# GpSimd zeroes the query buffer's lower rows, and the first layer norm is made in two halves

## The chip, the cores and the metric

One Trainium2 chip, one core of it. The time is the device time of one execution in microseconds (us). The kernel is launched once and does everything on that core.

## What is computed

The input x has 8 sequences of 512 tokens of 128 numbers (float32). Four sublayers follow one another, each as x = x + f(layernorm(x)): a linear attention with 16 heads, a mixture of 8 experts, a causal softmax attention whose heads share one key and value, and a filter in frequency space. Only the first is touched by the steps below:

```python
def _layernorm(x, axis=-1, eps=1e-05):
    m = jnp.mean(x, axis=axis, keepdims=True)
    v = jnp.var(x, axis=axis, keepdims=True)
    return (x - m) / jnp.sqrt(v + eps)
...
    x = x + _L0_attn_ref(_layernorm(x, axis=-1), L0_attn_w, L0_attn_w_out)
    x = x + _L0_ffn_ref(_layernorm(x, axis=-1), L0_ffn_router_w, L0_ffn_w1, L0_ffn_b1, L0_ffn_w2, L0_ffn_b2)
    x = x + _L1_attn_ref(_layernorm(x, axis=-1), L1_attn_w_attn, L1_attn_w_proj)
    x = x + _L1_ffn_ref(_layernorm(x, axis=-1), L1_ffn_w_freq_real, L1_ffn_w_freq_imag, L1_ffn_bias)
```

## The kernel before, in words

Each engine has its own list of instructions, written by hand in one order, and semaphores tie the lists together. B is 8 sequences, P 128 partitions, NT 4 tiles of 128 tokens for each sequence, D 128.

**Start.** SyncE issues the loads of x (four sequences, then the constants, then the other four; lines 184 to 190) and then of the expert weights. ScalarE issues ten loads of small weights (L214). GpSimd's first work is `start_signals` (L176 to L182): it raises 110 semaphores one by one, in two lots, with s_started raised to 1 (LIN) after the first lot and to 2 (ALL) after the second. VectorE zeroes the lower 64 partitions of two buffers, `kTm` (L2134) and `qT` (L2135). These are used only by the third sublayer, hundreds of microseconds later. The instruction for `qT` writes 12288 words of four bytes in each of 64 partitions.

**The first layer norm.** VectorE then makes mean and variance of all 8 sequences, two sequences at a time (`dve_sequences`: eight BATCH_NORM_STATS2 at L292, a wait, eight BATCH_NORM_AGGREGATE at L297; four times). It adds epsilon for all of them in one small instruction that writes the tile `sd` (L306). ScalarE, which has loaded the table of the square root while it waited (an `act_preset` at L269 is a one-element activation that makes the table load happen), takes the root (L316) and then loads the table of the exponential. VectorE goes on with `prep_dve`: it copies the transposed weights out of PSUM (L247 to L253), waits for TensorE's next products (L233 to L236) and copies these (L256, L258). Only then it takes the reciprocal (L310) and the product of it with minus the mean, the tile `shift1` (L2144). ScalarE's `xln` (L464, normalised x, four tiles) waits for that.

**The linear attention.** TensorE transposes `xln` of sequence 0 (L601), ScalarE copies the result (L470), TensorE multiplies by the weights (L611), ScalarE makes `kx` and `qv` out of it (L481, L482), VectorE the largest query of each head, `qmax` (L367), GpSimd adds to the keys (L533), and TensorE sums the keys (L621, L622). Then there is one turn for each sequence (`dve_lin_turn`, `act_lin_turn`, `pe_lin_turn`, `pool_lin_turn`), turn b doing the sums of sequence b and the start of sequence b+1. `act_lin_turn` of turn b ends with the `xln` of sequence b+2. GpSimd's list from `lin_pool` on begins with L533 of sequence 0.

Of the kernel before, what the change touches and what calls it, by code (L numbers as in the profile page):

```python
# [17 lines left out]
ALU = mybir.AluOpType  # L18
# [3 lines left out]
P = 128  # L22
# [26 lines left out]
def build(nc, x_in, w_qkv, w_out, router_w, w1, b1, w2, b2, w_attn, w_proj, wf_re, wf_im, f_bias,  # L49
# [15 lines left out]
    with ExitStack() as ctx:  # L65
# [177 lines left out]
        def prep_dve(dve):  # L243
            dve.wait_ge(s_c.sem, s_c.total(16))
            nc.vector.tensor_copy(ident_bf[:, :], ident).then_inc(s_idb.sem, 1)
            dve.wait_ge(s_prep_t.sem, s_prep_t.total(1))
# [25 lines left out]
        ln_ve, ln_sd, ln_rstd = signal("ln_var_eps"), signal("ln_std"), signal("ln_rstd")  # L272

        class LayerNorm:


            def __init__(self, tag, nth):
                self.nth = nth
# [20 lines left out]

            def dve_rstd(self, dve):  # L300
                self.dve_var_eps(dve, B)
                self.dve_inverse(dve)

            def dve_var_eps(self, dve, turns):
                dve.wait_ge(self.mv.sem, self.mv.total(turns))
                nc.vector.tensor_scalar(sd[:, :, :], mv[:, :, :, 1], EPS, None, ALU.add).then_inc(self.ve.sem, 1)  # L306

            def dve_inverse(self, dve):
                dve.wait_ge(self.sd.sem, self.sd.total(self.nth))
                nc.vector.reciprocal(rstd[:, :, :], sd[:, :, :]).then_inc(self.rstd.sem, 1)  # L310
                dve.wait_ge(self.rstd.sem, self.rstd.total(self.nth))

            def act_std(self, act):
                act_preset(act, ACT.Sqrt)
                act.wait_ge(self.ve.sem, self.ve.total(self.nth))
                nc.scalar.activation(sd[:, :, :], sd[:, :, :], ACT.Sqrt).then_inc(self.sd.sem, 1)  # L316

        ln1, ln2, ln3, ln4 = (LayerNorm(f"ln{n}", n) for n in range(1, 5))

# [192 lines left out]
        def lin_act(act):  # L512
# [337 lines left out]
        def route_act(act):  # L850
            act_preset(act, ACT.Exp)
            act.wait_ge(s_shift.sem, s_shift.total(2))
            act_route_xln(act, 0, 0)
# [475 lines left out]

        def dve_inverse(dve, lo, hi, nth):  # L1330
            dve.wait_ge(ln_sd.sem, ln_sd.total(nth))
            nc.vector.reciprocal(rstd[:, lo:hi, :], sd[:, lo:hi, :]).then_inc(ln_rstd.sem, 1)
            dve.wait_ge(ln_rstd.sem, ln_rstd.total(nth))

        def act_std(act, lo, hi, nth, preset=True):
            if preset:
                act_preset(act, ACT.Sqrt)
            act.wait_ge(ln_ve.sem, ln_ve.total(nth))
            nc.scalar.activation(sd[:, lo:hi, :], sd[:, lo:hi, :], ACT.Sqrt).then_inc(ln_sd.sem, 1)

        def dve_filter_xln(dve, j):
# [80 lines left out]
        def dve_end_xln(dve, half):  # L1422
            part, to = x_sb[:, SEQ[B - 1], end_tiles(half), :], fx[:, (B - 1) % 2, end_tiles(half), :]
            token = lambda a: a.unsqueeze(2).broadcast_to([P, END_TILES, D])
            dve.wait_ge(ln_sd.sem, ln_sd.total(7 + half))
            nc.vector.reciprocal(rstd[:, B - 1, end_tiles(half)], sd[:, B - 1, end_tiles(half)]).then_inc(ln_rstd.sem, 1)
            nc.vector.tensor_tensor(to, part, token(mv[:, B - 1, end_tiles(half), 0]), ALU.subtract).then_inc(f_c.sem, 1)
            dve.wait_ge(ln_rstd.sem, ln_rstd.total(7 + half))
            dve.wait_ge(f_c.sem, f_c.at(B - 2, half + 1))
# [13 lines left out]
        def act_end_std(act, half):  # L1443
            act.wait_ge(ln_ve.sem, ln_ve.total(7 + half))
            nc.scalar.activation(sd[:, B - 1, end_tiles(half)], sd[:, B - 1, end_tiles(half)], ACT.Sqrt).then_inc(ln_sd.sem, 1)
# [51 lines left out]
        def act_end_xln(act):  # L1497
            act.wait_ge(s_shift.sem, s_shift.total(5))
            act.wait_ge(f_xTp.sem, f_xTp.at(B - 4, 1))
# [106 lines left out]
        def dve_turn(dve, b, tail=True, middle=True, front=True):  # L1606
            for s in range(STEPS):
                for place in PLACES:
# [14 lines left out]
                    if b == B - 1 and (s, place) == (0, "A"):  # L1623
                        dve_inverse(dve, 0, IN_LAST_TURN, 5)
                    if b == B - 1 and place == "A" and s in XLN_AT:
# [10 lines left out]
        def mqa_dve(dve):  # L1636
# [4 lines left out]
            dve_moe_add(dve, last_scatter(SEQ[1]), SEQ[1])  # L1641
            dve_inverse(dve, 0, 1, 3)
            dve_ln3_shift(dve, 0, 1)
# [10 lines left out]
            dve_max(dve, 0, range(2), bank_at_start)  # L1654
            dve_inverse(dve, 1, B, 4)
            dve_ln3_shift(dve, 1, B)
# [8 lines left out]
            dve_var_eps(dve, ln4, B - 2, B - 1)  # L1665
            dve_inverse(dve, B - 2, B - 1, 6)
            dve_end_shift(dve)
# [107 lines left out]
        def act_turn(act, b, tail=True, middle=True, front=True):  # L1775
            for s in range(STEPS):
# [10 lines left out]
                if (b, s) == (STD_TURN, STD_STEP):  # L1787
                    act_std(act, 0, IN_LAST_TURN, 5)
                    act_preset(act, ACT.Exp)
# [17 lines left out]

        def mqa_act(act):
            act_std(act, 0, 1, 3)
            act.wait_ge(s_shift.sem, s_shift.total(3))  # L1810
            act_xln(act, 0)
# [6 lines left out]
            act_first_kT(act, 0)  # L1818
            act_std(act, 1, B, 4, preset=False)
            act_preset(act, ACT.Exp)  # L1820
            act.wait_ge(s_shift.sem, s_shift.total(4))
            act_xln(act, 1)
# [286 lines left out]
        @block.scalar  # L2109
        def _(act):  # L2110
            prep_act(act)
            act.wait_ge(s_started, LIN)
            act.wait_ge(s_c.sem, s_c.total(16))
            ln1.act_std(act)
            act_preset(act, ACT.Exp)
            lin_act(act)
            act.wait_ge(s_started, ALL)
            ln2.act_std(act)
            route_act(act)
            moe_act(act)  # L2120
            mqa_act(act)
# [91 lines left out]
```

## Time and profile before

| | before |
|---|---|
| median of 3 runs | 795.57 us (793.87 to 795.86) |
| span of the profiled execution | 801.9 us |
| TensorE busy in it | 644.6 us (80%) |
| VectorE busy | 548.5 us (68%) |
| ScalarE busy | 353.9 us (44%) |
| GpSimd busy | 361.2 us (45%) |

The only time of the profiled execution itself that is at hand is its span, from its first to its last instruction, and that is 6.3 us more than the median of the three runs. In the chain of work that ended last, the shares of the span are TensorE 45%, VectorE 20%, GpSimd 13%, waiting for nothing that the profile shows 12%. The first sublayer fills about the first 205 us. In the names of the engines, PE is TensorE's matmul, PEld its weight load, DVE VectorE, ACT ScalarE, POOL GpSimd and SP SyncE; a "q" behind a name is its queue. An arrow in brackets names what ended the idle time of the engine just before the row.

### The profile page before, as it was taken

The page shows a single profiled execution, that of the slowest core. Times are in us where ns is not written, and L with a number is a line of the kernel's source. Part 1 is how long each engine was busy: PE and PEld are TensorE (multiplying, and loading weights), DVE is VectorE, ACT ScalarE, POOL GpSimd, SP SyncE. Part 2 cuts the span into 40 slices and gives each one's busy share as a digit, 9 for nine tenths or more (in the row PEclk, how much of TensorE's full clock was granted, in tenths as well). Part 3 has the DMA queues.
Part 4 walks back from the last instruction along what each step waited for, and adds up shares of the span by engine and source line. Part 5 has one row for each costly group of instructions (what it writes and reads, how often), then busy time and mean ns, then how long its engine had stood idle before and what let it go on. Part 6 is the DMA issues. An engine that isn't in the chain of part 4 may idle for free.

```text
span 801.9 us, 14622 instructions
## 1 busy us (share of the span) xinstructions
PE 644.6 (80%) x4312; PEld 398.9 (50%) x4345; DVE 548.5 (68%) x1808; ACT 353.9 (44%) x764; POOL 361.2 (45%) x513
## 2 busy tenths in 40 slices
PE   1489898997206699999795569899999999999795
PEld 1246666664103478877584223454545454544453
DVE  8378888888691133243336797889898989898454
ACT  0323232320711222233231205776777777767883
POOL 0176555552007587788862102434434344333342
PEclk9999999999657799999997667999999999999998
DMA  9300000000231222223324440203131221300011
GB/s 297 106 1 1 0 1 0 0 1 1 78 106 49 32 43 41 41 42 43 44 25 102 52 59 4 60 16 50 26 41 31 34 41 25 50 15 2 17 54 40
DMA packets 42937, 33.51 MB, mean 42 GB/s; under 512 B 4144, under 2 KB 39520, under 8 KB 42864
## 3 DMA queue, kind: packets, MB, share of 16 engines
q1 hardware_dynamic: 32528, 24.62, 14.3%
q0 software_dynamic: 8992, 7.38, 6.4%
q8 instruction: 35, 0.57, 0.3%
q10 hardware_dynamic: 1344, 0.62, 0.3%
q14 instruction: 38, 0.31, 0.2%
HBM read 13.87 MB, written 8.91 MB: 28 GB/s over the span
## 4 chain that ended last, share of the span: by engine, by line
PE 45%; DVE 20%; POOL 13%; issue 12%; ACT 3%; DMA 2%; SPq 1%; DVEq 0%; ACTq 0%; POOLq 0%
PE bank L1982 8%; DVE masked L1574 7%; POOL x_dram L950 7%; POOL x_row L943 6%; PE wide L1969 5%; PE wide L639 4%; PE bank L1914 3%; PE bank L611 3%; PE wide L640 3%; PE bank L1121 2%; DVE st L292 2%; DVE mx L1574 2%; DVE prod L389 2%; PE wide L621 1%; PE bank L1994 1%
## 5 line engine op out<-in xcount | busy, mean ns | idle before, releaser
L1761 ACT ACTIVATE pexp<-wide 128x512 f32<-128x512 f32 (+2 forms) x384 | 181.3, 535 | 73.4 <-PE wide L1969 70.2
L1685 POOL TENSOR_SCALAR_AFFINE_SELECT pexp<-pexp 128x256 f32<-128x256 f32 x256 | 106.1, 418 | 185.7 <-ACT pexp L1761 183.7
L1574 DVE CUSTOM_DVE_ANT_0 masked<-bank,mask_qk 128x384 f32<-128x384 f32 (+3 forms) x356 | 154.0, 481 | 18.6 <-PE bank L1914 17.7
L1969 PE MATMUL wide<-qT,kTe 128*128 128x256 bf16 (+3 forms) x501 | 119.7, 301 | 6.6 <-ACT pexp L1761 2.5
L1092 ACT ACTIVATE hT<-wide,b1T 128x512 f32<-128x512 f32 x64 | 43.8, 687 | 147.1 <-PE wide L1112 112.8
L1914 PE MATMUL bank<-kTm,qT 128*128 128x384 bf16 (+3 forms) x348 | 87.1, 318 | 18.9 <-DVE mx L1574 9.4
L950 POOL DMA_INDIRECT x_dram<-yg,row_u x48 | 76.2, 1588 | 31.5 <-DVE yg L999 18.6
L1574 DVE CUSTOM_DVE_ANT_0 masked<-wide,mask_qk 128x256 f32<-128x256 f32 (+3 forms) x156 | 74.2, 498 | 17.8 <-PE wide L1914 17.8
L943 POOL DMA_INDIRECT x_row<-xln_dram,row_u x64 | 62.4, 975 | 52.8 <-DVE slot_tok L819 33.6
L1982 PE MATMUL bank<-pexp,vx 128*32 128x512 f32 (+3 forms) x1024 | 83.9, 439 | 0.5 <-POOL pexp L1685 0.5
L1121 PE MATMUL bank<-w_sb,hT 128*128 128x128 f32 x512 | 71.6, 283 | 5.0 <-issue 5.0
L1121 PEld LDWEIGHTS bank<-w_sb,hT 128*128 128x128 f32 x512 | 66.2, 197 | 17.2 <-issue 16.1
L565 POOL TENSOR_TENSOR kv<-kx,qv 128x1024 f32<-128x1024 f32 x32 | 62.4, 1951 | 24.2 <-PE wide L640 24.2
L1112 PE MATMUL wide<-xgT,w_sb 128*128 128x512 f32 x128 | 69.2, 628 | 2.8 <-DVE xgT L982 1.6
L1969 PEld LDWEIGHTS wide<-qT,kTe 128*128 128x128 bf16 x512 | 48.5, 99 | 41.5 <-ACT pexp L1761 21.6
L1914 PEld LDWEIGHTS bank<-kTm,qT 128*128 128x128 bf16 x356 | 30.8, 102 | 66.5 <-DVE mx L1574 48.4
L389 DVE TENSOR_TENSOR prod<-wide,qs 128x1024 f32<-128x1024 f32 x32 | 38.9, 1217 | 11.6 <-PE wide L640 9.0
L1982 PEld LDWEIGHTS bank<-pexp,vx 128*32 128x32 f32 x1024 | 25.9, 109 | 40.2 <-issue 28.4
L639 PE MATMUL wide<-kv,cst 128*128 128x512 f32 x64 | 35.7, 640 | 10.4 <-DVE prod L389 10.3
L1574 DVE DVE_READ_ACCUMULATOR2_ANT mx<- 128x1 f32 x512 | 42.6, 83 | 0.0
L996 DVE TENSOR_TENSOR yg<-bank,b2rep 128x512 f32<-128x512 f32 x16 | 11.1, 691 | 44.8 <-PE bank L1121 40.9
L398 DVE TENSOR_REDUCE y_in<-prod 128x128 f32<-128x1024 f32 x32 | 38.9, 1216 | 3.9 <-PE bank L664 3.4
(273 smaller groups left out, 1056.0 us busy)
## 6 DMA issues: line engine op xcount, KB each, us to landing
qT<-qp SPq DMA_DIRECT2D x144, 64.0 KB
x_sb<-in_L_attn_x SPq DMA_DIRECT2D x8, 256.0 KB, 6.7
w_sb<-in_L_ffn_w SPq DMA_DIRECT2D x1, 2048.0 KB, 13.3
xln_dram<-rx SPq DMA_DIRECT2D x8, 256.0 KB, 2.3
out_x<-x_sb SPq DMA_DIRECT2D x7, 256.0 KB, 2.3
x_dram<-x_sb SPq DMA_DIRECT2D x6, 256.0 KB, 3.6
x_sb<-x_dram SPq DMA_DIRECT2D x6, 256.0 KB, 2.8
x_row<-xln_dram,row_u POOLq DMA_INDIRECT x64
```

The source lines that it names most:

```text
L565: nc.gpsimd.tensor_tensor(kv[:, k % 2, :].rearrange("p (h m l) -> p h m l", l=L, m=L), kx[:, par, k, :].rearrange("p (h l) -> p h l", l=L) ...
L639: nc.tensor.matmul(wide[:, 0:512], tri, kv[:, k % 2, 0:512], start=True, stop=True)
L943: nc.gpsimd.indirect_dma_start(out=x_row[:, e % 2, b, :], out_offset=None, in_=xln_dram, in_offset=bass.IndirectOffsetOnAxis(ap=row_u[:, b ...
L950: nc.gpsimd.indirect_dma_start(out=x_dram, out_offset=bass.IndirectOffsetOnAxis(ap=row_u[:, b * E + e:b * E + e + 1], axis=0), in_=yg[:, e ...
L1112: nc.tensor.matmul(psH[n % 3], w1_sb[:, e, c * P:(c + 1) * P], xgT[:, half, :], start=True, stop=True).then_inc(m_hp, 1)
L1121: ins = nc.tensor.matmul(psYe[half][:, j * D:(j + 1) * D], hT[:, half, c, j * P:(j + 1) * P], w2_sb[:, e, c, :], start=c == 0, stop=c == H ...
L1574: ins = nc.vector.tensor_tensor_reduce(out=masked[:, n % 4, at], in0=bank_of(n)[:, at], in1=mask_qk[:, T - w:T], scale=1.0, scalar=LEAST, ...
L1685: nc.gpsimd.affine_select(out=pexp[:, at, :, 0:P], in_=pexp[:, at, :, 0:P], pattern=[[0, 2], [1, P]], compare_op=ALU.is_ge, fill=0.0, base ...
L1761: nc.scalar.activation(pexp[:, exp_slot(b, 2 * step + h // 2), h % 2:h % 2 + nh, 0:w], scores_bank(b, m)[:, 0:nh * w].rearrange("p (h t) - ...
L1914: ins = nc.tensor.matmul(place[:, hh * w:(hh + 1) * w], qT[:, b % QB, h + hh, k * P:(k + 1) * P], kTm[:, b % 2, 0:w], start=True, stop=True)
L1969: ins = nc.tensor.matmul(scores_bank(b, m)[:, hh * w:(hh + 1) * w], kTe[:, par, j * P:(j + 1) * P], qT[:, b % QB, 4 * qd + h + hh, j * P:T ...
L1982: ins = nc.tensor.matmul(psO[32 * g:32 * g + 32, j * P:T], vx[:, b % 2, j, :], pexp[:, exp_slot(b, 2 * step + g // 2), g % 2, 0:w], start= ...
```

## The change

Five edits.

1. The zeroing of `qT` moves from VectorE to GpSimd, behind `start_signals` and ahead of `lin_pool`, with a wait for its end behind it.
2. VectorE makes the statistics of the first four sequences only, then their epsilon, their reciprocal and their shift, and then does `prep_dve`.
3. The statistics and the epsilon of the other four sequences come behind `prep_dve`, ahead of the linear attention. The copy of the identity into bf16 (L245) moves from the head of `prep_dve` to just behind them.
4. The root of the second half stands on ScalarE between its turns 0 and 1, with a load of the root's table ahead of it and of the exponential's behind it. VectorE takes the second half's reciprocal and shift between its turns 0 and 1. ScalarE waits for that shift at the head of each pass of its loop over later turns.
5. TensorE waits for the eighth copy of `prep_dve` (L258) before it sums the keys of sequence 0. Numbers of later waits follow the new counts.

```diff
         def prep_dve(dve):
-            dve.wait_ge(s_c.sem, s_c.total(16))
-            nc.vector.tensor_copy(ident_bf[:, :], ident).then_inc(s_idb.sem, 1)
             dve.wait_ge(s_prep_t.sem, s_prep_t.total(1))
...
+            def dve_var_eps(self, dve, turns, lo, hi):
                 dve.wait_ge(self.mv.sem, self.mv.total(turns))
+                nc.vector.tensor_scalar(sd[:, lo:hi, :], mv[:, lo:hi, :, 1], EPS, None, ALU.add).then_inc(self.ve.sem, 1)
+
+        def dve_inverse(dve, lo, hi, name):
+            dve.wait_ge(ln_sd.sem, ln_sd.total(NORM[name]))
+            nc.vector.reciprocal(rstd[:, lo:hi, :], sd[:, lo:hi, :]).then_inc(ln_rstd.sem, 1)
+            dve.wait_ge(ln_rstd.sem, ln_rstd.total(NORM[name]))
...
@@ lin_dve
             dve_lin_turn(dve, 0, 0, tail=False)
+            dve_inverse(dve, B // 2, B, "ln1_second")
+            dve_shift_of_mean(dve, B // 2, B)
             dve_lin_turn(dve, 1, 1)
@@ lin_act
             act_lin_turn(act, 0, 0, tail=False)
+            act_std(act, B // 2, B, "ln1_second")
+            act_preset(act, ACT.Exp)
             act_lin_turn(act, 1, 1)
             with nc.scalar.Fori(1, B // 2 - 1) as i:
+                act.wait_ge(s_shift.sem, s_shift.total(2))
@@ lin_pe
                 pe_lin_qkv(pe, 0, k)
+            pe.wait_ge(s_prep_v.sem, s_prep_v.total(8))
             pe_lin_key_sums(pe, 0, 0, first=True)
@@ scalar
-            ln1.act_std(act)
+            act_std(act, 0, B // 2, "ln1_first")
             act_preset(act, ACT.Exp)
@@ vector
             nc.vector.memset(kTm[64:P, :, :], 0.0).then_inc(s_zero.sem, 1)
-            nc.vector.memset(qT[64:P, :, :, :], 0.0).then_inc(s_zero.sem, 1)
             dve.wait_ge(s_started, LIN)
-            for i in range(B // 2):
-                if i % 2 == 0:
-                    dve.wait_ge(s_x[i // 2].sem, s_x[i // 2].total(16 * B // 2))
-                ln1.dve_sequences(dve, i, 2)
-            ln1.dve_var_eps(dve, B // 2)
+            dve.wait_ge(s_x[0].sem, s_x[0].total(16 * B // 2))
+            ln1.dve_sequences(dve, 0, 2)
+            ln1.dve_sequences(dve, 1, 2)
+            ln1.dve_var_eps(dve, 2, 0, B // 2)
+            dve_inverse(dve, 0, B // 2, "ln1_first")
+            dve_shift_of_mean(dve, 0, B // 2)
             prep_dve(dve)
-            ln1.dve_inverse(dve)
-            nc.vector.scalar_tensor_tensor(out=shift1[:, :, :], in0=mv[:, :, :, 0], scalar=-1.0, in1=rstd[:, :, :],
-                                           op0=ALU.mult, op1=ALU.mult).then_inc(s_shift.sem, 1)
+            dve.wait_ge(s_x[1].sem, s_x[1].total(16 * B // 2))
+            ln1.dve_sequences(dve, 2, 2)
+            ln1.dve_sequences(dve, 3, 2)
+            ln1.dve_var_eps(dve, 4, B // 2, B)
+            nc.vector.tensor_copy(ident_bf[:, :], ident).then_inc(s_idb.sem, 1)
             lin_dve(dve)
@@ gpsimd
             start_signals(pool)
+            nc.gpsimd.memset(qT[64:P, :, :, :], 0.0).then_inc(s_zero.sem, 1)
+            pool.wait_ge(s_zero.sem, s_zero.total(2))
             lin_pool(pool)
```

## Rows read from the trace of the kernel before

**Rows 1.** Chain of work that ended last, first 30 us: start, length (us), work.

```profile
24.03 0.18 DVE sd L306
27.31 0.20 DVE shift L2144
29.24 1.13 PE bank L601 x4
```

**Rows 2.** Timeline of VectorE at the start: start us, length us, instruction.

```profile
3.96 10.30 DVE L2135 MEMSET qT<- 64x12288 uint32 x1 [2.51 <-issue]
14.29 1.65 DVE L292 BATCH_NORM_STATS2 st<-x_sb 128x6 f32<-128x128 f32 x8
...
18.43 0.64 DVE L297 BATCH_NORM_AGGREGATE mv<-st 128x2 f32<-128x6 f32 x8
...
24.26 0.55 DVE L247 COPY wqT<-bank 128x384 f32<-128x384 f32 x1
...
24.90 0.41 DVE L250 COPY a<-bank 128x256 f32<-128x256 f32 x1
```

**Rows 3.** Timeline of ScalarE and TensorE at the start.

```profile
15.13 0.63 PE L231 MATMUL bank<-cst,wf_sb 128*128 128x128 f32 x2
...
24.25 0.23 ACT L316 ACTIVATE sd<-sd 128x32 f32<-128x32 f32 x1 [13.11 <-DVE sd L306]
...
25.79 0.20 ACT L269 ACTIVATE preset<-cst 128x1 f32<-128x1 f32 x1
...
26.38 0.43 PE L236 MATMUL bank<-wqT,cst 128*128 128x8 f32 x2
...
27.54 1.65 ACT L464 ACTIVATE xln<-x_sb,shift,rstd 128x128 f32<-128x128 f32 x4 [1.54 <-DVE shift L2144]
```

**Rows 4.** Instructions on tile x_sb, first 2.9 us: the first four loads.

```profile
L186 SPq DMA_DIRECT2D x_sb<-in_L_attn_x x4: 442/500/507, 0.8 to 2.4; - x4
...
DMA to landing us min/median/max: 3.6/4.6/5.5
```

**Rows 5.** Line 182, GpSimd's last raise of a semaphore at the start.

```profile
L182 POOLq EVENT_SEMAPHORE  x1: 17/17/17, 9.8 to 9.8; - x1
```

**Rows 6.** GpSimd's groups by shape: instruction, count, busy us, mean ns, idle before.

```profile
L565 POOL TENSOR_TENSOR kv<-kx,qv 128x1024 f32<-128x1024 f32 x32 | 62.4, 1951 | 24.2 <-PE wide L640 24.2
...
L533 POOL TENSOR_SCALAR kx<-kx 128x512 f32<-128x512 f32 x8 | 11.9, 1493 | 39.9 <-ACT qv L482 36.7 <-ACT kx L481 3.1
...
L1559 POOL COPY kTe<-kTm 72x512 bf16<-72x512 bf16 x8 | 4.9, 608 | 1.3 <-ACT kTm L1806 1.3
...
L844 POOL IOTA tokens<- 128x512 int32 x1 | 0.6, 560 | 12.6 <-DVE x_sb L410 12.6
...
L2201 POOL MEMSET const-float32-0.0<- 128x1 f32 x1 | 0.1, 99 | 0.3 <-issue 0.3
```

**Rows 7.** Timeline in the third sublayer, 518.1 to 519.2 us: VectorE casts and GpSimd.

```profile
518.21 0.20 DVE L1527 CAST mp<-mx 128x64 bf16<-128x64 f32 x1
...
518.67 0.41 POOL L1685 TENSOR_SCALAR_AFFINE_SELECT pexp<-pexp 128x256 f32<-128x256 f32 x1 [0.85 <-ACT pexp L1761]
518.70 0.43 DVE L1527 CAST mp<-mx 128x64 bf16<-128x64 f32 x1
```

**Rows 8.** Line 1328 (min/median/max ns), and its longest instance in the timeline.

```profile
L1328 DVE TENSOR_SCALAR sd<-mv x4: 164/175/233, 430.1 to 783.0; 128x4 f32<-128x4 f32 x2, 128x28 f32<-128x28 f32 x1, 128x24 f32<-128x24 f32 x1
...
430.07 0.23 DVE L1328 TENSOR_SCALAR sd<-mv 128x4 f32<-128x4 f32 x1
```

**Rows 9.** Timeline, 37 to 69 us: idle time of three engines before these instructions.

```profile
37.22 1.51 POOL L533 TENSOR_SCALAR kx<-kx 128x512 f32<-128x512 f32 x1 [36.72 <-ACT qv L482]
37.26 0.69 DVE L367 TENSOR_REDUCE qmax<-qv 128x64 f32<-128x512 f32 x1 [9.76 <-ACT qv L482]
...
64.02 0.60 ACT L470 ACTIVATE xT<-bank 128x512 f32<-128x512 f32 x1 [6.74 <-PE bank L601]
...
68.52 0.69 DVE L367 TENSOR_REDUCE qmax<-qv 128x64 f32<-128x512 f32 x1 [1.02 <-ACT qv L482]
```

More of the change, by code:

```diff
@@ L272, in build, with __init__ @@
         ln_ve, ln_sd, ln_rstd = signal("ln_var_eps"), signal("ln_std"), signal("ln_rstd")
+        NORM = {name: n + 1 for n, name in enumerate(
+            ("ln1_first", "ln1_second", "ln2", "ln3_first", "ln3_rest", "ln4_six", "ln4_seventh", "ln4_end_0", "ln4_end_1"))}
         class LayerNorm:
-            def __init__(self, tag, nth):
-                self.nth = nth
+            def __init__(self, tag):
                 self.six = signal(f"{tag}_bn_stats")
@@ L298, in dve_sequences_of, with dve_shift_of_mean, act_std @@
                 ins.then_inc(self.mv.sem, 1)
[L300 to L304, printed above, removed]
+            def dve_var_eps(self, dve, turns, lo, hi):
                 dve.wait_ge(self.mv.sem, self.mv.total(turns))
[L306 to L313, printed above, removed]
+                nc.vector.tensor_scalar(sd[:, lo:hi, :], mv[:, lo:hi, :, 1], EPS, None, ALU.add).then_inc(self.ve.sem, 1)
[3 more added lines that the diff above has]
+            dve.wait_ge(ln_rstd.sem, ln_rstd.total(NORM[name]))
+        def dve_shift_of_mean(dve, lo, hi):
+            nc.vector.scalar_tensor_tensor(out=shift1[:, lo:hi, :], in0=mv[:, lo:hi, :, 0], scalar=-1.0, in1=rstd[:, lo:hi, :],
+                                           op0=ALU.mult, op1=ALU.mult).then_inc(s_shift.sem, 1)
+        def act_std(act, lo, hi, name, preset=True):
+            if preset:
                 act_preset(act, ACT.Sqrt)
-                act.wait_ge(self.ve.sem, self.ve.total(self.nth))
-                nc.scalar.activation(sd[:, :, :], sd[:, :, :], ACT.Sqrt).then_inc(self.sd.sem, 1)
-        ln1, ln2, ln3, ln4 = (LayerNorm(f"ln{n}", n) for n in range(1, 5))
+            act.wait_ge(ln_ve.sem, ln_ve.total(NORM[name]))
+            nc.scalar.activation(sd[:, lo:hi, :], sd[:, lo:hi, :], ACT.Sqrt).then_inc(ln_sd.sem, 1)
+        ln1, ln2, ln3, ln4 = (LayerNorm(f"ln{n}") for n in range(1, 5))
         A = lambda name, per=1: signal("lin_" + name, per)
@@ L760, in route_dve @@
         def route_dve(dve):
-            nc.vector.scalar_tensor_tensor(out=shift1[:, :, :], in0=mv[:, :, :, 0], scalar=-1.0, in1=rstd[:, :, :],
-                                           op0=ALU.mult, op1=ALU.mult).then_inc(s_shift.sem, 1)
+            dve_shift_of_mean(dve, 0, B)
             rows = lg[:, :, :, :].rearrange("p b k e -> p (b k) e")
@@ L851, in route_act @@
             act_preset(act, ACT.Exp)
-            act.wait_ge(s_shift.sem, s_shift.total(2))
+            act.wait_ge(s_shift.sem, s_shift.total(3))
             act_route_xln(act, 0, 0)
@@ L1328, in dve_var_eps @@
             nc.vector.tensor_scalar(sd[:, lo:hi, :], mv[:, lo:hi, :, 1], EPS, None, ALU.add).then_inc(ln_ve.sem, 1)
[L1330 to L1339, printed above, removed]
         def dve_filter_xln(dve, j):
@@ L1424, in dve_end_xln @@
             token = lambda a: a.unsqueeze(2).broadcast_to([P, END_TILES, D])
-            dve.wait_ge(ln_sd.sem, ln_sd.total(7 + half))
+            dve.wait_ge(ln_sd.sem, ln_sd.total(NORM["ln4_end_0"] + half))
             nc.vector.reciprocal(rstd[:, B - 1, end_tiles(half)], sd[:, B - 1, end_tiles(half)]).then_inc(ln_rstd.sem, 1)
             nc.vector.tensor_tensor(to, part, token(mv[:, B - 1, end_tiles(half), 0]), ALU.subtract).then_inc(f_c.sem, 1)
-            dve.wait_ge(ln_rstd.sem, ln_rstd.total(7 + half))
+            dve.wait_ge(ln_rstd.sem, ln_rstd.total(NORM["ln4_end_0"] + half))
             dve.wait_ge(f_c.sem, f_c.at(B - 2, half + 1))
@@ L1443, in act_end_std @@
         def act_end_std(act, half):
-            act.wait_ge(ln_ve.sem, ln_ve.total(7 + half))
+            act.wait_ge(ln_ve.sem, ln_ve.total(NORM["ln4_end_0"] + half))
             nc.scalar.activation(sd[:, B - 1, end_tiles(half)], sd[:, B - 1, end_tiles(half)], ACT.Sqrt).then_inc(ln_sd.sem, 1)
@@ L1497, in act_end_xln @@
         def act_end_xln(act):
-            act.wait_ge(s_shift.sem, s_shift.total(5))
+            act.wait_ge(s_shift.sem, s_shift.total(6))
             act.wait_ge(f_xTp.sem, f_xTp.at(B - 4, 1))
@@ L1623, in dve_turn @@
                     if b == B - 1 and (s, place) == (0, "A"):
-                        dve_inverse(dve, 0, IN_LAST_TURN, 5)
+                        dve_inverse(dve, 0, IN_LAST_TURN, "ln4_six")
                     if b == B - 1 and place == "A" and s in XLN_AT:
@@ L1641, in mqa_dve @@
             dve_moe_add(dve, last_scatter(SEQ[1]), SEQ[1])
-            dve_inverse(dve, 0, 1, 3)
+            dve_inverse(dve, 0, 1, "ln3_first")
             dve_ln3_shift(dve, 0, 1)
@@ L1654, in mqa_dve @@
             dve_max(dve, 0, range(2), bank_at_start)
-            dve_inverse(dve, 1, B, 4)
+            dve_inverse(dve, 1, B, "ln3_rest")
             dve_ln3_shift(dve, 1, B)
@@ L1665, in mqa_dve @@
             dve_var_eps(dve, ln4, B - 2, B - 1)
-            dve_inverse(dve, B - 2, B - 1, 6)
+            dve_inverse(dve, B - 2, B - 1, "ln4_seventh")
             dve_end_shift(dve)
@@ L1787, in act_turn @@
                 if (b, s) == (STD_TURN, STD_STEP):
-                    act_std(act, 0, IN_LAST_TURN, 5)
+                    act_std(act, 0, IN_LAST_TURN, "ln4_six")
                     act_preset(act, ACT.Exp)
@@ L1808, in mqa_act @@
         def mqa_act(act):
-            act_std(act, 0, 1, 3)
-            act.wait_ge(s_shift.sem, s_shift.total(3))
+            act_std(act, 0, 1, "ln3_first")
+            act.wait_ge(s_shift.sem, s_shift.total(4))
             act_xln(act, 0)
@@ L1818, in mqa_act @@
             act_first_kT(act, 0)
-            act_std(act, 1, B, 4, preset=False)
+            act_std(act, 1, B, "ln3_rest", preset=False)
             act_preset(act, ACT.Exp)
-            act.wait_ge(s_shift.sem, s_shift.total(4))
+            act.wait_ge(s_shift.sem, s_shift.total(5))
             act_xln(act, 1)
@@ L1830, in mqa_act @@
                 act_turn(act, b, tail=b > 0, middle=b + 1 < B, front=b + 2 < B)
-            act_std(act, B - 2, B - 1, 6)
+            act_std(act, B - 2, B - 1, "ln4_seventh")
             act_quad(act, B - 1, NQ - 1)
@@ L2117, in _ @@
             act.wait_ge(s_started, ALL)
-            ln2.act_std(act)
+            act_std(act, 0, B, "ln2")
             route_act(act)
@@ L2134, in _ @@
             nc.vector.memset(kTm[64:P, :, :], 0.0).then_inc(s_zero.sem, 1)
-            nc.vector.memset(qT[64:P, :, :, :], 0.0).then_inc(s_zero.sem, 1)
             dve.wait_ge(s_started, LIN)
-            for i in range(B // 2):
-                if i % 2 == 0:
-                    dve.wait_ge(s_x[i // 2].sem, s_x[i // 2].total(16 * B // 2))
-                ln1.dve_sequences(dve, i, 2)
-            ln1.dve_var_eps(dve, B // 2)
-            prep_dve(dve)
-            ln1.dve_inverse(dve)
-            nc.vector.scalar_tensor_tensor(out=shift1[:, :, :], in0=mv[:, :, :, 0], scalar=-1.0, in1=rstd[:, :, :],
-                                           op0=ALU.mult, op1=ALU.mult).then_inc(s_shift.sem, 1)
+            dve.wait_ge(s_x[0].sem, s_x[0].total(16 * B // 2))
[4 more added lines that the diff above has]
+            dve_shift_of_mean(dve, 0, B // 2)
+            prep_dve(dve)
+            dve.wait_ge(s_x[1].sem, s_x[1].total(16 * B // 2))
[3 more added lines that the diff above has]
+            nc.vector.tensor_copy(ident_bf[:, :], ident).then_inc(s_idb.sem, 1)
             lin_dve(dve)
             dve.wait_ge(s_started, ALL)
-            ln2.dve_rstd(dve)
+            ln2.dve_var_eps(dve, B, 0, B)
+            dve_inverse(dve, 0, B, "ln2")
             route_dve(dve)
```

## The prediction

> **What bounds the kernel now.** I read the chain of work that ended last first, because every edit sits in the first 66 us and what matters is whether that stretch is on the chain. It is: the epsilon `sd` at 24.03, the shift at 27.31, TensorE's transposes of sequence 0 at 29.24 [rows 1]. From there each step hands over to the next, so whatever moves the transposes moves the end by as much. The timeline of VectorE then shows why they are so late: the zeroing of `qT` ends at 14.26, and the four lots of statistics follow without a gap, two lots from 14.29 to 19.07 (4.78 us) [rows 2], the other two until the epsilon. VectorE is the bound from 1.5 to 24.2 us. The recorded start of the zeroing, 3.96, is to be read with care; only its end is used.
>
> **What the data allows.** The fourth load of x is issued at 2.4 and the longest of the four lands 5.5 us after its issue, so the first four sequences are there at 7.9 [rows 4]. Without the zeroing the two lots run from 7.9 to 12.7. The epsilon would be written by 12.9 (its 0.18 of [rows 1]).
>
> **From the epsilon to the transposes, in the new order.** Call v the moment when the epsilon is written (24.21 before). Two legs start there. ScalarE: in the profile the root starts at 24.25 and the exponential's preset ends at 25.99, which is v + 1.78 [rows 3]; before, that lay under `prep_dve`, now it doesn't. `xln` takes 1.65, and TensorE follows 0.05 behind its end: v + 3.5. VectorE: reciprocal and shift end about v + 0.8 (the root ends at v + 0.27, the shift takes 0.20 [rows 1], the reciprocal I estimate at 0.3), the copies L247 to L250 take 1.05 (24.26 to 25.31) [rows 2], and TensorE's products end 1.50 behind the last of these (25.31 to 26.81) [rows 2, 3]: v + 3.35. ScalarE's leg is the later one. Before, the transposes started at v + 5.03. So they start at v + 3.5, but not before 18.4: the copies can't start before TensorE's first lot of transposes ends at 15.76, and 15.8 + 1.05 + 1.50 is 18.35 [rows 3].
>
> If v is 12.9, the floor of 18.4 holds and the gain is 29.24 - 18.4 = **10.8 us**. What decides is whether the epsilon can be written at 12.9.
>
> **GpSimd's zeroing.** It starts when the signals are raised, at 9.8 [rows 5], say 9.9. The trace has no such instruction of this size on GpSimd. IOTA is nearest, as it only writes: 560 ns for 512 words; less the 0.10 us of a one-element memset, that is 0.90 ns a word, and 12288 words take 11.1 us [rows 6]. I take that. With the fixed part counted in, 1.09 ns and 13.4 us. Bounds: VectorE's own row of 10.3 us below [rows 2], and above, the copy's 1.19 ns (608/512), 14.6 us; the two-input product's 1.91 ns (1951/1024), 23.4 us; the tensor-scalar's 2.92 ns, 35.8 us [rows 6]. A zeroing written as 24576 half-words at 0.90 ns would take 22. The Trainium skill, "GPSIMD Engine Reference", section 3.1 "Elementwise — side-by-side cycle accounting", gives 1.03 cycles an element for the simplest bodies, at 1.2 GHz an estimate of 10.5 us, with which the sum below would be 5.3 in place of 4.7. By the rows it ends at 21.0, between 20.2 and 24.5 in the likely part; the far ends are kept for the rivals.
>
> Is it hidden? Behind it in GpSimd's list stands the work on the keys of sequence 0, for which TensorE waits. Before, GpSimd had been idle for 36.7 us when that began at 37.22 [rows 9], 8.0 us behind the transposes. With these at 18.4 it would be wanted at 26.4. An end at 21.0 is hidden; one behind 26.4 delays everything by the excess.
>
> **The epsilon beside it.** At 12.7 GpSimd is in the midst of that one long instruction, and the epsilon is a tensor-scalar from SBUF to SBUF. In the third sublayer a cast of 64 elements from SBUF to SBUF takes 0.20 us alone; one that starts 0.03 behind a GpSimd instruction takes 0.43 and ends at 519.13, which is 0.05 behind the end of that instruction [rows 7]. It didn't share, it waited for the end. And the instruction in question, an epsilon of 4 columns, took 233 ns against 164 at 430.07, while GpSimd was issuing an indirect DMA [rows 8]. So I take it that the epsilon stands until the zeroing is over: v = 21.0 + 0.05, and the transposes start at 24.55.
>
> The Trainium skill, "SBUF — State Buffer", section "Who interferes with whom", says the same more sharply: copy, cast and tensor-scalar on VectorE can use both port pairs, one of which is GpSimd's, whoever comes first holds it for its whole instruction, and the other is blocked. This trace agrees for the cast (0.43 against 0.20 us); no row here shows it for an instruction that only writes. If GpSimd's writes did not count, the sum would be the 10.8 us above.
>
> **The sum.** 29.24 - 24.55 = 4.7 us. Check by its parts: the zeroing off VectorE and two lots of statistics behind the start would be worth 14.26 - 7.9 = 6.4 and 24.03 - 19.1 = 4.9, together 11.3; the order of shift and `prep_dve` 1.5 (5.03 against 3.5); the stall takes back 21.05 - 12.9 = 8.15. 11.3 + 1.5 - 8.15 = 4.7.
>
> **Edits costed at nothing.** *Second half's statistics:* 4.8 us and 0.4 of epsilon and identity copy, behind `prep_dve`, which ends near v + 3.6; done by v + 8.8. `qmax` is wanted 8.0 us behind the transposes, v + 11.5: VectorE idled 9.76 us there [rows 9]. Cover left, 2.7 us. *Root between ScalarE's turns:* two table loads of 1.3, two presets and the root, 3.4 us, into an idle time of 6.74 that the copy at 64.02 ended [rows 9]; 3.3 are left. *Reciprocal and shift between VectorE's turns:* 0.5 us ahead of the first product of turn 1, behind which VectorE stood idle for 1.02 us until ScalarE had `qv` for the next `qmax` at 68.52 [rows 9]. 0.5 us are left; without that idle time it would cost 0.5. *TensorE's new wait:* for a copy done at about v + 3.6, ahead of a sum wanted at v + 13. *The waits in ScalarE's loop:* always met, a few hundredths each. *First epsilon's 16 columns instead of 32:* nothing. No DMA is moved.
>
> The profiled execution spans 801.9 us; less 4.7 that is 797.2. It stands 6.3 above the median. The gain is in the first 30 us, so I take it from the median as it is: 795.57 - 4.7 = **790.9 us**. What a measurement of this kernel tells from no change is about 0.3%, 2.4 us.
>
> **Rivals.**
>
> *No stall.* A write-only instruction on GpSimd doesn't hold up the epsilon. For it: the rows show only GpSimd instructions that read too, or DMA issues; against it, the 233 ns. Gain 10.8, time **784.7**.
>
> *A slow zeroing, slower than before.* It takes 18.2 us or more (1.48 ns a word) and the epsilon waits for it. The gain is 15.8 minus the length: nothing is gained at 15.8 us (1.28 ns), and at the product's rate, 23.4 us, the epsilon is written at 33.35, the transposes start at 36.85 and the kernel takes 7.6 us more, **803.2**. For it: two of GpSimd's rows are above 1.28 ns a word, and IOTA's rate would be too if the zeroing went by half-words [rows 6]; against it, IOTA and the copy as they stand. Without the stall the same zeroing would end at 33.3, 3.9 us ahead of 37.22, still a gain.
>
> *Between.* The zeroing takes 13.4 to 18.2 us with the stall: within 2.4 us of before, **795**. The same if the second half's statistics lose their cover.
>
> **How the numbers follow.** Stall with a zeroing of 9.5 to 13.4 us, the forecast: 0.47 (gain 6.3 to 2.4). No stall: 0.27. Slow with stall: 0.13. Between: 0.13. Faster by over 0.3%: 0.47 + 0.27 = 0.74. Same 0.13, slower 0.13. The range leaves out the slow case and reaches to the others: 784 to 797. The forecast's own range is 789 to 793.
>
> **What the profile would show.** GpSimd's MEMSET of 12288 words from 9.9 to 21. VectorE's first two lots of statistics from 7.9 to 12.7. An `sd` row that ends 0.05 behind the MEMSET, however its start is recorded, and ScalarE's root idle until then. Transposes at 24.5. In the rival without a stall `sd` is at 12.7 and the transposes at 18.4. The gap between `sd` and transposes is 3.5 in the first case and 5.5 in the second, where TensorE's weights bound it. VectorE idle before `qmax`, ScalarE before its copy near 59. I am wrong if the MEMSET's rate is not near 0.9 ns, if `sd` comes ahead of its end, or if `qmax` of sequence 0 comes behind VectorE's own statistics.

## The result, and the profile after

The changed kernel takes **801.27 us** (median of 7 runs, 799.03 to 801.67) against 797.02 (7 runs, 793.87 to 798.72): the ratio is **1.0052, 95% interval 1.0037 to 1.0066**. It is 4.1 us slower, where 4.7 us less was forecast.

The chain of work that ended last in the changed kernel begins so (start, length in us, what):

```profile
2.38 5.78 DMA x_sb<-in_L_attn_x
...
8.27 1.65 DVE st L292 x8
...
12.42 0.65 DVE mv L297 x8
13.07 0.02 issue
13.09 17.45 DVE sd L302
30.54 0.02 issue
30.57 0.03 ACT sd L317
...
30.80 1.28 ACT L267
...
32.20 1.64 ACT xln L467 x4
33.84 0.04 issue
33.88 1.13 PE bank L607 x4
```

One row has taken the place of the zeroing and of two lots of statistics: the epsilon on 16 columns, 17.45 us long (before, with 32 columns, it took 0.18 [rows 1]). The transposes start at 33.88 in place of 29.24, 4.6 us later. Around it, in the timeline:

```profile
9.93 20.57 POOL L2154 MEMSET qT<- 64x24576 bf16 x1 [9.43 <-issue]
...
13.09 17.44 DVE L302 TENSOR_SCALAR sd<-mv 128x16 f32<-128x16 f32 x1
...
30.57 0.21 ACT L317 ACTIVATE sd<-sd 128x16 f32<-128x16 f32 x1 [19.07 <-DVE sd L302]
...
31.10 0.18 DVE L310 SCALAR_TENSOR_TENSOR shift<-mv,rstd 128x16 f32<-128x16 f32 x1
...
33.31 0.43 PE L236 MATMUL bank<-wqT,cst 128*128 128x8 f32 x2
...
40.88 1.51 POOL L539 TENSOR_SCALAR kx<-kx 128x512 f32<-128x512 f32 x1 [10.38 <-ACT kx L484]
40.93 0.69 DVE L368 TENSOR_REDUCE qmax<-qv 128x64 f32<-128x512 f32 x1 [1.87 <-ACT qv L485]
```

GpSimd's zeroing ends at 30.50 and the epsilon at 30.53, 0.03 behind it. The shape in the MEMSET row is the second thing to see: GpSimd writes 24576 elements of bf16, where VectorE's row had 12288 of uint32 for the same bytes [rows 2]. That is 0.837 ns an element. GpSimd stood idle for 10.38 us between its zeroing and the keys, so its own lateness cost nothing; only the epsilon paid.

Between turns 0 and 1, where the second half's shift now stands, the timeline shows another long row of a small instruction:

```profile
70.14 1.96 POOL L571 TENSOR_TENSOR kv<-kx,qv 128x1024 f32<-128x1024 f32 x1
70.14 0.24 DVE L306 RECIPROCAL rstd<-sd 128x16 f32<-128x16 f32 x1
...
70.42 1.71 DVE L310 SCALAR_TENSOR_TENSOR shift<-mv,rstd 128x16 f32<-128x16 f32 x1
...
72.05 1.21 DVE L390 TENSOR_TENSOR prod<-wide,qs 128x1024 f32<-128x1024 f32 x1
```

It takes 1.71 us against 0.18 for the same shape at 31.10, and ends at 72.13, 0.03 behind GpSimd's product.

**Where the two profiles can be compared.** In the last turn of the linear attention VectorE's long reciprocal starts at 184.81, against 180.63 before: 4.2 us later. The lateness isn't the same all the way. It is 4.6 us at the transposes and 3.7 at the keys (40.88 against 37.22), because TensorE's eight products on the weights took 4.62 us against 5.59, at a granted clock of 1.00 in both profiles; why is open. It is 4.3 at VectorE's denominator `den` (46.58 against 42.25), behind TensorE's sums of the keys, for which the granted clock was 0.60 (42.4 to 46.6) against 0.69 (38.8 to 42.3). It is 4.1 at ScalarE's copy that stands just ahead of the second shift (68.11 against 64.02). But the span of the changed kernel's profile is 797.4, 4.5 us shorter than the 801.9 of before. Busy time by stretch, the two numbers behind the engines being the granted clock of TensorE and the DMA share; before:

```profile
60.00:180.00 120.00, 108.30 (x566) 73.05 (x565) 103.12 (x140) 34.74 (x92) 71.19 (x49) 1.00 0.00 1
186.00:192.00 6.00, 6.00 (x30) 4.22 (x29) 3.09 (x3) 0.60 (x1) 2.09 (x2) 0.72 0.00 0
262.00:278.00 16.00, 9.84 (x38) 6.67 (x37) 2.87 (x5) 3.22 (x5) 8.64 (x8) 0.68 0.19 29
```

and after:

```profile
64.00:184.00 120.00, 108.29 (x565) 73.02 (x564) 104.69 (x141) 35.25 (x94) 71.22 (x49) 1.00 0.00 1
190.00:196.00 6.00, 6.00 (x37) 4.57 (x38) 4.73 (x5) 0.60 (x1) 3.37 (x2) 1.00 0.00 0
264.00:280.00 16.00, 16.00 (x98) 11.73 (x97) 5.79 (x10) 5.39 (x8) 12.95 (x11) 1.00 0.30 44
```

The stretches up to 184 do the same work in the same time. Behind them the profiled execution of before falls back in two places. By GpSimd's IOTA it has lost 1.7 us (205.68 against 208.19, so that the changed kernel is only 2.5 us late there); the second pair of rows lies in that stretch, with a mean granted clock of 0.72 against 1.00. It loses another 8.2 us between two lots of transposes in the mixture of experts (256.55 and 272.29, against 259.03 and 266.54). The third pair of rows overlaps it: TensorE did 38 products against 98, at 0.68 against 1.00, and between 262 and 270 it stood idle for 5 us without waiting for anything that the profile shows. What held up that one execution isn't shown. So the two spans can't be compared; the experiments are read by ratios of medians, and by landmarks up to the last long reciprocal of the linear attention. The profiled execution of after took 799.34 us for its span of 797.4, so what lies around a span is 1.9 us.

### The profile page after: what moved, and what is told of

It reads as the page before. It is cut to its first block, busy times and chain, and to the rows that moved or that the text cites. A ratio compares the mean times of both kernels' runs of the same rounds, so it can differ in the third digit from the quotient of the medians.

```text
span 797.4 us, 14666 instructions
## 1 busy us (share of the span) xinstructions
PE 640.5 (80%) x4345; PEld 395.5 (50%) x4345; DVE 557.4 (70%) x1810; ACT 357.0 (45%) x769; POOL 382.8 (48%) x514
## 3 DMA queue, kind: packets, MB, share of 16 engines
q1 hardware_dynamic: 32528, 24.62, 14.3%
## 4 chain that ended last, share of the span: by engine, by line
PE 44%; DVE 22%; POOL 14%; issue 12%; ACT 3%; DMA 2%; SPq 1%; DVEq 0%; ACTq 0%; POOLq 0%
PE bank L1977 8%; POOL x_row L949 7%; DVE masked L1569 7%; POOL x_dram L956 6%; PE wide L1964 5%; PE bank L1909 4%; PE wide L645 3%; PE wide L646 3%; PE bank L617 3%; DVE sd L302 2%; DVE st L292 2%; DVE prod L390 2%; DVE mx L1569 2%; PE bank L1127 2%; PE bank L1989 2%
## 5 line engine op out<-in xcount | busy, mean ns | idle before, releaser
L1569 DVE CUSTOM_DVE_ANT_0 masked<-bank,mask_qk 128x384 f32<-128x384 f32 (+3 forms) x356 | 153.9, 481 | 18.4 <-PE bank L1909 17.5
L1964 PE MATMUL wide<-qT,kTe 128*128 128x256 bf16 (+3 forms) x512 | 122.0, 302 | 4.8 <-ACT pexp L1756 2.5
L1909 PE MATMUL bank<-kTm,qT 128*128 128x384 bf16 (+3 forms) x356 | 89.9, 320 | 18.1 <-DVE mx L1569 9.0
L1127 PE MATMUL bank<-w_sb,hT 128*128 128x128 f32 x512 | 69.8, 280 | 0.0
L1118 PE MATMUL wide<-xgT,w_sb 128*128 128x512 f32 x128 | 67.6, 615 | 1.6 <-DVE xgT L988 1.6
L1909 PE MATMUL wide<-kTm,qT 128*128 128x256 bf16 (+3 forms) x156 | 42.4, 323 | 2.2 <-DVE mx L1569 1.9
```

Source lines behind the costliest of these rows:

```text
L1118: nc.tensor.matmul(psH[n % 3], w1_sb[:, e, c * P:(c + 1) * P], xgT[:, half, :], start=True, stop=True).then_inc(m_hp, 1)
L1127: ins = nc.tensor.matmul(psYe[half][:, j * D:(j + 1) * D], hT[:, half, c, j * P:(j + 1) * P], w2_sb[:, e, c, :], start=c == 0, stop=c == H ...
L1569: ins = nc.vector.tensor_tensor_reduce(out=masked[:, n % 4, at], in0=bank_of(n)[:, at], in1=mask_qk[:, T - w:T], scale=1.0, scalar=LEAST, ...
L1909: ins = nc.tensor.matmul(place[:, hh * w:(hh + 1) * w], qT[:, b % QB, h + hh, k * P:(k + 1) * P], kTm[:, b % 2, 0:w], start=True, stop=True)
L1964: ins = nc.tensor.matmul(scores_bank(b, m)[:, hh * w:(hh + 1) * w], kTe[:, par, j * P:(j + 1) * P], qT[:, b % QB, 4 * qd + h + hh, j * P:T ...
```

## The experiments

The theory: the epsilon waits for the end of GpSimd's zeroing, and the zeroing costs by the element, 24576 of them. Rivals: its length goes by the bytes; the epsilon waits for something else; the halves themselves cost the time. All ratios are to the kernel before, timed together with each. `sd` is the first epsilon; its end and the zeroing's, the start of sequence 0's transposes and the start of its keys are read from each timeline, in us.

| kernel | median us | ratio (95% interval) | zeroing ends | `sd` ends | transposes | keys |
|---|---|---|---|---|---|---|
| before | 797.0 | 1 | 14.3 | 24.2 | 29.24 | 37.22 |
| changed | 801.27 | 1.0052 (1.0037 to 1.0066) | 30.5 | 30.5 | 33.88 | 40.88 |
| by words | 791.25 | 0.9933 (0.9909 to 0.9956) | 20.3 | 20.3 | 23.65 | 31.62 |
| two-input epsilon | 791.45 | 0.9932 (0.9909 to 0.9955) | 30.5 | 12.9 | 18.11 | 30.80 |
| both of these | 786.09 | 0.9856 (0.983 to 0.9881) | 20.3 | 12.9 | 18.20 | 25.19 |
| halves only | 790.14 | 0.9915 (0.989 to 0.9939) | 14.3 | 19.3 | 22.64 | 30.44 |
| six pieces | 791.96 | 0.9933 (0.9912 to 0.9955) | 30.8 | 13.5 | 18.12 | 31.11 |
| zeroing only | 801.81 | 1.0063 (1.0046 to 1.008) | 30.5 | 30.6 | 35.49 | 42.77 |
| late, by words | 785.37 | 0.9864 (0.9846 to 0.9883) | 193.3 | 13.1 | 18.04 | 25.09 |
| shift earlier | 784.47 (one time) | | 20.3 | 12.8 | 17.98 | 25.39 |

### The zeroing by words

```diff
-            nc.gpsimd.memset(qT[64:P, :, :, :], 0.0).then_inc(s_zero.sem, 1)
+            nc.gpsimd.memset(qT[64:P, :, :, :].rearrange("p b h t -> p (b h t)").bitcast(U32), 0).then_inc(s_zero.sem, 1)
```

> The changed kernel, with GpSimd's zeroing written as 12288 four-byte words in place of 24576 two-byte ones; the same bytes. Theory (the epsilon waits for the end of GpSimd's instruction, and that instruction costs by the element, 0.837 ns): it takes 10.3 us, from 9.9 to 20.2, sd is written at 20.3, the transposes start 3.34 behind that, at 23.6, against 29.24 before and 33.88 in the changed kernel; the kernel takes 5.6 us less than before (ratio 0.993). Rival (it costs by the byte): 20.6 us again, sd at 30.5, ratio 1.005 as in the changed kernel. Rival (the epsilon doesn't wait for the zeroing but for something else): a zeroing of 10.3 us, but sd still at 30.5.

Its timeline:

```profile
9.93 10.33 POOL L2154 MEMSET qT<- 64x12288 uint32 x1 [9.43 <-issue]
...
13.03 7.26 DVE L302 TENSOR_SCALAR sd<-mv 128x16 f32<-128x16 f32 x1
...
23.65 1.11 PE L607 MATMUL bank<-cst,xln 128*128 128x128 f32 x4
```

Half the elements, half the time: 10.33 us, 0.841 ns each. The epsilon ends at 20.29, 0.03 behind. The cost goes by the element, and the stall follows the zeroing's end. The kernel is now faster than before, by 0.7%.

### An epsilon with two inputs

```diff
-                nc.vector.tensor_scalar(sd[:, lo:hi, :], mv[:, lo:hi, :, 1], EPS, None, ALU.add).then_inc(self.ve.sem, 1)
+                nc.vector.scalar_tensor_tensor(out=sd[:, lo:hi, :], in0=mv[:, lo:hi, :, 1], scalar=EPS, in1=mv[:, lo:hi, :, 1],
+                                               op0=ALU.add, op1=ALU.max).then_inc(self.ve.sem, 1)
```

> The changed kernel, zeroing as it is (20.6 us), but the epsilon is added by a scalar-tensor-tensor that reads the variance twice, max(v + eps, v), which gives the same numbers. Theory (only a VectorE instruction that uses both ports at its output too is held by an instruction of GpSimd that only writes): sd is written at 13.3, the transposes start at 18.4; the identity's cast waits for the zeroing's end at 30.5, the keys (wanted at 26.4) too; they start at 30.6 against 37.2 before and 40.9 in the changed kernel: 6.6 us less than before (ratio 0.992). Rival (any VectorE instruction of small size at that place waits, or two inputs wait too): sd at 30.5, ratio 1.005.

Its timeline:

```profile
9.93 20.57 POOL L2155 MEMSET qT<- 64x24576 bf16 x1 [9.43 <-issue]
...
12.69 0.18 DVE L302 SCALAR_TENSOR_TENSOR sd<-mv 128x16 f32<-128x16 f32 x1
...
13.15 0.25 DVE L307 RECIPROCAL rstd<-sd 128x16 f32<-128x16 f32 x1 [0.28 <-ACT sd L318]
...
15.70 0.56 DVE L245 COPY wqT<-bank 128x384 f32<-128x384 f32 x1 [2.09 <-PE bank L231]
...
23.27 0.17 DVE L302 SCALAR_TENSOR_TENSOR sd<-mv 128x16 f32<-128x16 f32 x1
23.37 7.22 DVE L2143 CAST ident_bf<-cst 128x128 bf16<-128x128 f32 x1
...
25.42 5.17 DVE L369 TENSOR_REDUCE qmax<-qv 128x64 f32<-128x512 f32 x1
30.80 1.51 POOL L540 TENSOR_SCALAR kx<-kx 128x512 f32<-128x512 f32 x1 [0.30 <-POOL qT L2155]
```

In the midst of the zeroing the new epsilon takes 0.18 and 0.17 us. The cast of the identity, which still has one input and both its sides in SBUF, takes the stall over, 7.22 us to 30.59, and GpSimd's keys come directly behind the zeroing. So it is the form of the instruction that decides, not its place. One input and both sides in SBUF are not enough to be held: the reciprocal has them too and takes 0.25 us inside the zeroing, and the statistics read one SBUF tile and keep their 1.65. The copies out of PSUM aren't held either (0.56 us for the largest, 0.55 before). The edit changes the kind of instruction together with the number of inputs, and no run separates the two. What is left of the zeroing is now GpSimd's own lateness, as the changed kernel would have it without the stall.

### Both

> Both of the edits: zeroing by words, and the two-input epsilon. Theory: sd at 13.3, zeroing over at 20.2, transposes at 18.4, the keys at 26.4, nothing waits for GpSimd: 10.8 us less than before (ratio 0.986). Rival (two inputs wait too): as with the words alone, transposes at 23.6, ratio 0.993.

Measured: 0.9856. `sd` takes 0.17 us at 12.72, the transposes start at 18.20 and the keys at 25.19, with GpSimd idle for 4.92 us before them. TensorE's last product on the weights starts at 17.92 and is recorded until 18.35, while ScalarE's `xln` was done at 16.2: the weights bound the start now.

### The halves alone

```diff
             nc.vector.memset(kTm[64:P, :, :], 0.0).then_inc(s_zero.sem, 1)
+            nc.vector.memset(qT[64:P, :, :, :], 0.0).then_inc(s_zero.sem, 1)
...
-            nc.gpsimd.memset(qT[64:P, :, :, :], 0.0).then_inc(s_zero.sem, 1)
-            pool.wait_ge(s_zero.sem, s_zero.total(2))
```

> The changed kernel with the zeroing left on VectorE as before: the halves alone. Theory: the zeroing ends at 14.26, two lots of statistics at 19.07, sd at 19.3, transposes 3.34 behind, at 22.6: 6.6 us less than before (ratio 0.992). Rival (the halves themselves cost what was lost, by the table loads, the second shift between turns 0 and 1 or the late statistics): the ratio is at or above 1, with the keys no earlier than before.

Measured: 0.9915; `sd` at 19.11 takes 0.17 us, the transposes start at 22.64. Edits 2 to 5 of the change are worth 6.8 us by themselves. They were not the loss.

### Six pieces

```diff
-            nc.gpsimd.memset(qT[64:P, :, :, :], 0.0).then_inc(s_zero.sem, 1)
+            for b in range(QB):
+                for h in (0, HEADS // 2):
+                    ins = nc.gpsimd.memset(qT[64:P, b, h:h + HEADS // 2, :], 0.0)
+            ins.then_inc(s_zero.sem, 1)
```

> The changed kernel, its zeroing of 24576 half-words cut into six instructions of 4096, with the tensor-scalar epsilon. Theory (VectorE is held until the end of the GpSimd instruction that is running, and gets its turn there): the pieces end at 13.4, 16.8, 20.3, ... 30.5; sd is written at 13.5, the transposes start at 18.4, the keys at 30.6; about 6.6 us less than before (ratio 0.992), as with the two-input epsilon. Rival (GpSimd's queue keeps the port from one instruction to the next): sd at 30.5, ratio 1.005.

Its timeline, the six pieces merged into one row:

```profile
9.94 20.87 POOL L2156 MEMSET qT<- 64x4096 bf16 x6 [9.43 <-issue]
...
13.07 0.40 DVE L302 TENSOR_SCALAR sd<-mv 128x16 f32<-128x16 f32 x1
...
23.27 0.57 DVE L302 TENSOR_SCALAR sd<-mv 128x16 f32<-128x16 f32 x1
23.36 0.56 DVE L2142 CAST ident_bf<-cst 128x128 bf16<-128x128 f32 x1
```

The pieces are recorded with 3.50 to 3.60 us each. The first ends at 13.45 and the epsilon at 13.47. The fourth ends at 23.81, the second epsilon at 23.84 and the cast at 23.92. VectorE gets its turn at the seam, and the six pieces cost 0.3 us more than one.

### The zeroing alone

The kernel before, with edit 1 and nothing else.

```diff
             nc.vector.memset(kTm[64:P, :, :], 0.0).then_inc(s_zero.sem, 1)
-            nc.vector.memset(qT[64:P, :, :, :], 0.0).then_inc(s_zero.sem, 1)
...
             start_signals(pool)
+            nc.gpsimd.memset(qT[64:P, :, :, :], 0.0).then_inc(s_zero.sem, 1)
+            pool.wait_ge(s_zero.sem, s_zero.total(2))
             lin_pool(pool)
```

> The kernel before with edit 1 alone: the zeroing on GpSimd (24576 half-words), the layer norm in one piece. Theory: the statistics run early, but the epsilon waits for the end of the zeroing at 30.5; the transposes start 5.03 behind, at 35.6 against 29.2; 6.3 us more than before (ratio 1.008). Rival (the loss of the changed kernel comes with the halves): ratio at or below 1.

Its timeline:

```profile
19.74 10.81 DVE L306 TENSOR_SCALAR sd<-mv 128x32 f32<-128x32 f32 x1
19.83 10.78 DVE L245 CAST ident_bf<-cst 128x128 bf16<-128x128 f32 x1
```

The statistics of all 8 sequences are done at 19.7, and the epsilon waits until 30.55. The transposes start at 35.49, 6.25 later than before, and the last long reciprocal at 186.64, 6.0 later. The kernel takes 5.0 us more (1.0063) where 6.3 were expected; the interval, 3.7 to 6.4 us, holds both. The halves win 1.6 us of that back at the transposes in the changed kernel (33.88), the difference in order that the prediction put at 1.5.

### The zeroing late, by words

```diff
             start_signals(pool)
-            nc.gpsimd.memset(qT[64:P, :, :, :], 0.0).then_inc(s_zero.sem, 1)
-            pool.wait_ge(s_zero.sem, s_zero.total(2))
             lin_pool(pool)
+            pool.wait_ge(a_kv.sem, a_kv.at(B - 1, NT))
+            nc.gpsimd.memset(qT[64:P, :, :, :].rearrange("p b h t -> p (b h t)").bitcast(U32), 0).then_inc(s_zero.sem, 1)
+            pool.wait_ge(s_zero.sem, s_zero.total(2))
```

> The changed kernel with the tensor-scalar epsilon as it is, and the zeroing by words moved on GpSimd's list behind its last product of the linear attention, where it idled for 12.6 us. Theory: nothing is held at the start, sd at 13.1, transposes at 18.4, keys at 26.4, the zeroing of 10.3 us fits into the idle time; 10.8 us less than before (ratio 0.986). Rival (the zeroing holds something there or makes GpSimd's next work late): ratio nearer to 0.993, and a long row on VectorE near 190 us or a later IOTA that something waits for.

Its timeline of GpSimd:

```profile
182.98 10.34 POOL L2156 MEMSET qT<- 64x12288 uint32 x1
195.59 0.56 POOL L850 IOTA tokens<- 128x512 int32 x1 [2.27 <-DVE x_sb L411]
```

Measured: 0.9864, the same as "both" within the intervals, with the epsilon in its plain form. GpSimd still waits 2.27 us for its next work. No VectorE row between 183 and 193 is longer than at the other turns.

### The second shift where GpSimd is idle

"Both", and in turn 0:

```diff
                 dve_lin_qsum(dve, b + 1)
+                if not tail:
+                    dve_inverse(dve, B // 2, B, "ln1_second")
+                    dve_shift_of_mean(dve, B // 2, B)
                 dve_lin_den(dve, b + 1)
...
-            dve_inverse(dve, B // 2, B, "ln1_second")
-            dve_shift_of_mean(dve, B // 2, B)
             dve_lin_turn(dve, 1, 1)
```

> Zeroing by words and two-input epsilon, and the reciprocal and shift of the second half moved up on VectorE, ahead of the denominator of turn 0, where GpSimd stands idle. Theory (the shift reads two SBUF tiles and waits for a GpSimd instruction that reads SBUF): the shift takes 0.18 us there in place of 1.70; in the time it is worth at most 0.1 us, as TensorE waited little for the product behind it. Rival (the shift is slow for another reason): 1.7 us there too.

In "both" the shift and the product behind it were:

```profile
54.82 1.71 DVE L311 SCALAR_TENSOR_TENSOR shift<-mv,rstd 128x16 f32<-128x16 f32 x1
...
56.44 1.21 DVE L391 TENSOR_TENSOR prod<-wide,qs 128x1024 f32<-128x1024 f32 x1
...
57.80 1.10 PE L646 MATMUL wide<-kv,cst 128*128 128x512 f32 x2
```

and here:

```profile
49.00 0.17 DVE L311 SCALAR_TENSOR_TENSOR shift<-mv,rstd 128x16 f32<-128x16 f32 x1
...
54.97 1.22 DVE L391 TENSOR_TENSOR prod<-wide,qs 128x1024 f32<-128x1024 f32 x1
...
57.98 1.02 PE L647 MATMUL wide<-kv,cst 128*128 128x512 f32 x2
```

The shift takes 0.17 us and the product comes 1.5 us earlier. Little of that reaches TensorE's sums, for which the product frees the bank. This profile runs 0.2 us behind the other at the transposes of sequence 1 (32.93 against 32.72) and still at these sums (57.98 against 57.80). From the next pair of sums on it is 0.1 us behind (58.84 against 58.74), and so it is at the last long reciprocal (169.33 against 169.22). So the stall is real, and by these landmarks of one profile each it costs 0.1 us, the most that was expected. The single time, 784.47, can't show that: the five times of "both" run from 782.61 to 787.31.

## Why the prediction was wrong, step by step

**The step that failed** is the length of GpSimd's zeroing. The prediction took 12288 elements, as VectorE's row has them, at 0.90 ns, and got 11.1 us. The rate was near: 0.837 measured. The count was not: on GpSimd the instruction has 24576 elements of bf16, 20.57 us. "A zeroing written as 24576 half-words at 0.90 ns would take 22" stood among the bounds, and it was put into the 0.13 of the slow rival. Its formula, gain = 15.8 minus the length, gives -4.8 us for 20.57; measured were -4.6 at the transposes and -4.1 in the time. The zeroing by words, 10.33 us, gives 15.8 - 10.33 = 5.5, and the measured ratio of 0.9933 is 5.3 us. The forecast's sum was that of a kernel in which the zeroing is written by words. Why the one engine's instruction came out by words and the other's didn't, for the same call on the same bf16 tile, is not in any trace; only the shapes are.

**The steps that held.** That the epsilon stands until the zeroing's end: shown (17.4, 7.3 and 10.8 us by the zeroing's end in three kernels, 0.18 without). The Trainium skill, "SBUF — State Buffer", section "Who interferes with whom", says that a VectorE instruction with two SBUF inputs contends with a GpSimd instruction that reads SBUF and not with one that only writes. The trace agrees on both sides: the two-input epsilon took 0.18 us inside the zeroing, the two-input shift 1.71 beside GpSimd's product. From `sd` to the transposes, 3.5 forecast, 3.34 to 3.36 measured in the changed kernel, by words and with the halves alone. First two lots of statistics from 7.9, measured 8.27 in the changed kernel. The floor set by TensorE's weights, 18.4 forecast, 18.0 to 18.2 measured. No stall at all, 10.8 us forecast, 11.5 and 10.8 measured (0.9856 and 0.9864 of 797). Cover of ScalarE's second root: 3.3 forecast; it was idle for 3.60 before the copy at 68.11. Cover of the late statistics: 2.7 forecast, 1.87 measured, as TensorE's products of sequence 0 took 4.6 us from first to last in place of 5.6.

**What the prediction did not have.** The second shift was costed at 0.5 us with its reciprocal; the shift alone took 1.71, and 0.17 where GpSimd was idle. VectorE's idle time of 1.02 us, out of which the prediction had 0.5 left, was gone: the next `qmax` followed at once, at 73.18. It still cost only 0.1 us, as TensorE had other products to do meanwhile: the changed kernel was 4.1 us late at ScalarE's copy ahead of it (68.11 against 64.02) and 4.2 at the product behind TensorE's next sums (75.40 against 71.21). The prediction also let whatever moves the transposes move the end by as much; 4.6 us there were 4.2 at the last long reciprocal, by TensorE's products and sums of sequence 0 as shown above.

The range, 784 to 797, reached to the gain of a missing stall and left out the slow case, which had a chance of 0.13. Two of GpSimd's rows and the count by half-words spoke for that case. The weight given to it was small for an instruction of which the trace before showed no instance of any size on that engine.

## What to carry to other kernels

A small tensor-scalar or cast on VectorE from SBUF to SBUF, placed beside a long GpSimd instruction, cost what was left of the long one here. A reciprocal, the statistics and copies out of PSUM did not; a copy from SBUF to SBUF stood nowhere beside the zeroing and isn't tested. So look at every VectorE instruction in the time of the one that is moved to GpSimd, not only at what waits for its result. Cut the long instruction, put it where VectorE has none of the held kinds, or give the small one a second input if GpSimd only writes; each of the three took the epsilon's stall away here (to 0.40, 0.17 and 0.18 us), though with the second input alone the cast was held in its place. And when an instruction moves to another engine, count its elements anew: the same bytes were 12288 elements on one and 24576 on the other, and that alone was the difference between 0.7% faster and 0.5% slower.

## What the runs showed of the hardware

The record of a held instruction begins long before its work can, and so does that of the one behind it: the `qmax` of the two-input kernel is recorded with 5.17 us from 25.42, behind a cast that is recorded until 30.59. Its own work is 0.69 us. Read the end of such rows. GpSimd's zeroing costs 0.837 to 0.841 ns an element for two-byte and four-byte elements alike, on 64 partitions, and 0.86 in pieces of 4096 elements. A held VectorE instruction ended 0.02 to 0.11 us behind the GpSimd instruction that held it. The second shift took 1.70 to 1.71 us in each of the seven kernels that have it between the turns, also where no zeroing was on GpSimd (the halves alone).
